# Dense matrices of a graph network: counts and first weight part in one product, three pairs of PSUM banks in turn

## The reference, cut to what matters

```python
h = relu(layernorm(x)); x = x + segment_sum(edge_weight[:, None] * h[src], dst)        # layer 0
h = relu(layernorm(x)); x = x + L1(h, edge_attr_2, src, dst)                           # MLP on every edge
h = relu(layernorm(x)); x = x + relu(segment_sum(edge_weight[:, None] * (h @ W)[src], dst) + bias)
h = relu(layernorm(x))
for l in range(3):                                                                     # layer 3
    out = segment_sum(h[src] + edge_attr_128, dst) + h
    z = gelu(layernorm(out @ W1[l].T + b1[l]))
    h = gelu(layernorm(z @ W2[l].T + b2[l]) + h)
x = x + h
```

## Time and profile before

| | us |
|---|---|
| median of 3 runs | 5626.27 |
| lowest, highest | 5624.34, 5633.94 |
| the profiled execution | 5629.7 |
| its span, first to last instruction | 5627.9 |
| the stage that builds the matrices | 168 to 1364 |
| layer 1, edge by edge | 1420 to 3990 |
| layer 2, sums by the stored weight matrix | 3990 to 4250 |
| the last three layers | 4250 to 5628 |

### The profile page before, as it was taken

One profiled execution on the slowest core, in us unless ns is written; L12 is line 12 of the kernel. 1 busy time (PEld: TensorE's weight loads), 2 busy tenths in 40 slices (PEclk: granted clock), 3 DMA queues, 4 the chain that ended last, 5 costly groups with the idle time before them and its releaser, 6 DMA issues.

```text
span 5627.9 us, 139608 instructions
## 1 busy us (share of the span) xinstructions
PE 4909.3 (87%) x42810; PEld 4173.0 (74%) x42810; DVE 3168.0 (56%) x9378; ACT 1754.6 (31%) x3785; POOL 2089.6 (37%) x2575
## 2 busy tenths in 40 slices
PE   1899999998888888888888888659998999999998
PEld 1799999998777777777777777459996666666665
DVE  7899999996555555555555555630003444444444
ACT  2555555555111111111111111210001444445445
POOL 6211111111777777777777777000000111111000
PEclk8999999999999999999999999879998999999999
DMA  6344444444555555555555555037775554554554
GB/s 169 148 205 198 193 191 205 205 199 166 132 132 132 132 133 133 131 133 132 133 132 132 133 131 133 12 137 294 291 292 188 189 183 176 189 183 178 188 183 160
DMA packets 464598, 943.57 MB, mean 168 GB/s; under 512 B 107346, under 2 KB 395970, under 8 KB 426898
## 3 DMA queue, kind: packets, MB, share of 16 engines
q1 hardware_dynamic: 187778, 696.55, 32.9%
q0 software_dynamic: 58304, 121.69, 9.0%
q10 hardware_dynamic: 218448, 124.48, 8.2%
HBM read 691.90 MB, written 250.56 MB: 167 GB/s over the span
## 4 chain that ended last, share of the span: by engine, by line
PE 65%; issue 10%; POOL 9%; DVE 5%; DMA 4%; ACT 3%; DVEq 3%; ACTq 1%; POOLq 0%; SPq 0%
PE ps L1142 20%; PE ps L975 10%; PE ps L997 10%; POOL BIG L695 9%; PE ps L960 7%; PE ps L1075 4%; DMA BIG<-table,IDX 4%; PE ps L1073 4%; PE ps L1085 4%; PE ps L958 2%; DVEq L378 2%; PE ps L1074 1%; ACT ACC L805 1%; PE ps L1029 1%; DVE BIG L1482 1%
## 5 line engine op out<-in xcount | busy, mean ns | idle before, releaser
L695 POOL DMA_INDIRECT BIG<-table,IDX x1664 | 1615.9, 971 | 535.5 <-issue 470.3
L1491 DVE TENSOR_TENSOR ACC<-ACC,ps 128x257 f32 x1664 | 702.4, 422 | 588.9 <-PE ps L1085 571.1
L1073 PE MATMUL ps<-T,BIG 128*128 x3328 | 698.7, 293 | 342.0 <-DMA BIG<-table,IDX 194.5
L1073 PEld LDWEIGHTS ps<-T,BIG 128*128 128x128 f32 x3328 | 539.8, 200 | 458.0 <-issue 449.7
L1085 PE MATMUL ps<-BIG 128*128 128x257 f32 x3328 | 808.3, 385 | 0.0
L1075 PE MATMUL ps<-BIG,ident 128*128 128x128 f32 x3328 | 771.4, 315 | 0.0
L975 PE MATMUL ps<-H,ACC 128*128 128x128 f32 x4802 | 690.5, 284 | 0.0
L1085 PEld LDWEIGHTS ps<-BIG 128*128 128x128 f32 x3328 | 615.3, 195 | 73.6
L833 ACT ACTIVATE IDX<-SRC 128x4 int32 (+1 forms) x416 | 85.1, 205 | 1827.9 <-PE ps L1075 1144.3
L960 PE MATMUL ps<-T,BIG 128*128 128x98 bf16 x9408 | 633.0, 206 | 0.0
L958 PE MATMUL ps<-BIG 128*128 128x98 bf16 x3136 | 569.4, 207 | 70.1 <-ACT ACC L805 53.2
(11 more groups left out here) (233 smaller groups left out, 6318.9 us busy)
## 6 DMA issues: line engine op xcount, KB each, us to landing
weight_mat<-ACC SPq DMA_DIRECT2D x49, 3136.0 KB, 9.3
BIG<-weight_mat SPq DMA_DIRECT2D x49, 3136.0 KB, 10.2
BIG<-count_mat SPq DMA_DIRECT2D x73, 1568.0 KB, 6.5
REL_WT<-count_mat SPq DMA_DIRECT2D x72, 1568.0 KB, 6.6
count_mat<-BIG SPq DMA_DIRECT2D x49, 1568.0 KB, 12.8
BIG<-rel_tab ACTq DMA_DIRECT2D x416, 128.0 KB, 3.1
BIG<-in_edge_attr SPq DMA_DIRECT2D x832, 64.0 KB
BIG<-in_edge_attr ACTq DMA_DIRECT2D x832, 64.0 KB
```

The costliest lines, as they stand in the source:

```text
L695: pool.indirect_dma_start(G[:, q * QUAD + u, :], None, tables[1], bass.IndirectOffsetOnAxis(ap=IDX[:, q, u:u + 1], axis=0)).then_inc(gathe ...
L1073: pe.matmul(to, DT[:, q % 2, u * P:(u + 1) * P], T1[:, b[q * QUAD + u], :], start=True, stop=False)
L1491: dve.tensor_tensor(to, to, PS[4 + u][:, 0:2 * F + 1], ALU.add).then_inc(slots_free, 1)
```

## The change

- The count product and the first weight product of a window become one product of 196 columns. For this the plain one-hots and the three weighted ones of a slot lie in one tile, OH[slot], of four planes of 8 x 100 columns; the moving operand takes planes 0 and 1, 98 columns from each, 800 elements apart. The other two weight parts follow, 98 columns each.
- A group's results lie in a pair of banks (1024 words): window j has 256 words, counts in the first 98, weights in the next 98. Two windows share a bank, and only the first of the two clears it (start=True).
- Three pairs are used in turn, q % 3; group 15 takes pair 1, so that group 0 of the next block finds pair 0. Before group q TensorE waits for both copies of group q-3 (of q-2 for groups 1 and 15).
- The sums of block_products go to the fourth pair (PS[6] and PS[7]) in place of PS[2] and PS[3].
- OH[0] and OA lie in T1, OH[1] in BIG, where before OR and OA lay in BIG and OW in T1.

```diff
 WG = -(-WINDOWS // P)
 QW = 4
 RING = 4
+BANKS = 3
+WSLOT = 2 * P
 GROUPS = WPB // QW
 HW = 8
 HOTS = WPB // HW
...
         LOF = BIG[:, 0:WG * P].rearrange("p (g j c) -> p g j c", j=WN, c=HALF)
         CODEF = BIG[:, WG * P:2 * WG * P].rearrange("p (g j c) -> p g j c", j=WN, c=HALF)
         WF = T1f[:, NP - WG * P:NP].rearrange("p (g j c) -> p g j c", j=WN, c=HALF)
-        def hots(flat, slots, c):
-            return flat.bitcast(BF16).rearrange("p (s k w c) -> p s k w c", s=HSLOTS, k=slots, w=HW)
-
-        OA_, at = of_big(NP, HSLOTS * HW * P // 2)
-        OR_, at = of_big(at, HSLOTS * HW * WPAD // 2)
+        HOT = (1 + PARTS) * HW * WPAD // 2
+        OH1_, at = of_big(NP, HOT)
         WST_, at = of_big(at, 2 * (2 + PARTS) * WPB * 2)
         assert at <= 2 * NP - WINDOWS
-        OW_ = T1f[:, WINDOWS:WINDOWS + HSLOTS * PARTS * HW * WPAD // 2]
-        assert WINDOWS + HSLOTS * PARTS * HW * WPAD // 2 <= NP
-        OA, OR, OW = hots(OA_, 1, P), hots(OR_, 1, WPAD), hots(OW_, PARTS, WPAD)
+        OH0_ = T1f[:, WINDOWS:WINDOWS + HOT]
+        OA_ = T1f[:, WINDOWS + HOT:WINDOWS + HOT + HSLOTS * HW * P // 2]
+        assert WINDOWS + HOT + HSLOTS * HW * P // 2 <= NP
+        OA = OA_.bitcast(BF16).rearrange("p (s w c) -> p s w c", s=HSLOTS, w=HW)
+        OH = [flat.bitcast(BF16).rearrange("p (k w c) -> p k w c", k=1 + PARTS, w=HW) for flat in (OH0_, OH1_)]
         WST = WST_.bitcast(BF16).rearrange("p (a k w j) -> p a k w j", a=2, k=2 + PARTS, w=WPB)
         RELH0 = WG * WN * RUN * 3
...
         cmp = T2[:, 2 * SG * P:2 * SG * P + SG * (BLOCKS - 1)].rearrange("p (g b) -> p g b", b=BLOCKS - 1)
-        PS = [ctx.enter_context(nc.psum_tensor(f"ps{k}", [P, 512], FP32)) for k in range(8)]
+        PP = [ctx.enter_context(nc.psum_tensor(f"ps{k}", [P, 1024], FP32)) for k in range(4)]
+        PS = [PP[k // 2][:, k % 2 * 512:(k % 2 + 1) * 512] for k in range(8)]
         waits_passed = sem("waits_passed")
...
             return [(c, CHUNK if c < CHUNKS else 1, c % 2) for c in range(C1)]
+        def group_banks(q):
+
+            return PP[1 if q == GROUPS - 1 else q % BANKS]
+
+        def copies_needed(q):
+
+            return q + (2 if q in (1, GROUPS - 1) else 1)
+
         def again(v):
             return not isinstance(v, int) or v >= 2
...
             def store_block(b, par, i):
-                sp.wait_ge(group_out, (b + 1) * GROUPS + 4)
+                sp.wait_ge(group_out, (b + 1) * GROUPS + BANKS)
                 sp.dma_start(weight_mat[b, :, :], WB[par]).then_inc(mat_out[par], 16)
                 sp.dma_start(count_mat[b, :, :], CB[par]).then_inc(mat_out[par], 16)
...
                 which, n = k % 3, min(4 * P, WINDOWS - k // 3 * 4 * P)
                 act.wait_ge(wturned, k + 1)
                 act.activation((LO, CODE, WW)[which][:, k // 3 * 4 * P:k // 3 * 4 * P + n], PS[k % 4][:, 0:n], ACT.Copy).then_inc(wcopied, 1)
-            act.sem_inc(group_out, 4)
-            act.sem_inc(count_out, 2)
+            act.sem_inc(group_out, BANKS)
+            act.sem_inc(count_out, BANKS)
             act.sem_inc(wsum_used, 2)
...
                 act.wait_ge(wsum_ps, b + 1)
                 for q in range(GROUPS):
                     act.wait_ge(group_ps, b * GROUPS + q + 1 + RING)
-                    for pair, to, done in ((q % 2, CB[par], count_out), (4 + q % 4, WB[par], group_out)):
+                    for k, to, done in ((0, CB[par], count_out), (1, WB[par], group_out)):
+                        of = group_banks(q).rearrange("p (w z) -> p w z", z=WSLOT)[:, :, k * WCOLS:(k + 1) * WCOLS]
                         act.activation(
                             to.rearrange("p (h d) -> p h d", d=P)[:, :, q * QW * WN:(q + 1) * QW * WN].rearrange("p h (w j) -> p h w j", j=WN),
-                            PS[pair][:, 0:QW * WCOLS].rearrange("p (w h j) -> p h w j", w=QW, j=WN), ACT.Copy).then_inc(done, 1)
+                            of.rearrange("p w (h j) -> p h w j", j=WN), ACT.Copy).then_inc(done, 1)
             def copied_blocks():
                 block_pairs(act, group_copies)
                 act.wait_ge(mat_out[0], 32 * 25)
...
                     g, half = q // 2, q % 2
                     pe.wait_ge(hot_ready, (b + 2) * HOTS + g + 1)
-                    pe.wait_ge(count_out, b * GROUPS + q + 1)
-                    pe.wait_ge(group_out, b * GROUPS + q + 1)
+                    pe.wait_ge(count_out, b * GROUPS + copies_needed(q))
+                    pe.wait_ge(group_out, b * GROUPS + copies_needed(q))
                     for j in range(QW):
                         w = half * QW + j
-                        one = OA[:, g % HSLOTS, 0, w, :]
-                        pe.matmul(PS[q % 2][:, j * WCOLS:(j + 1) * WCOLS], one, OR[:, g % HSLOTS, 0, w, 0:WCOLS], start=True, stop=True)
-                        for k in range(PARTS):
-                            mm = pe.matmul(PS[4 + q % 4][:, j * WCOLS:(j + 1) * WCOLS], one, OW[:, g % HSLOTS, k, w, 0:WCOLS],
-                                           start=(k == 0), stop=(k == PARTS - 1))
+                        one, hot = OA[:, g % HSLOTS, w, :], OH[g % HSLOTS]
+                        to = group_banks(q)[:, j * WSLOT:j * WSLOT + 2 * WCOLS].rearrange("p (k c) -> p k c", k=2)
+                        pe.matmul(to, one, hot[:, 0:2, w, 0:WCOLS], start=(j % 2 == 0), stop=False)
+                        for k in range(1, PARTS):
+                            mm = pe.matmul(to[:, 1, :], one, hot[:, 1 + k, w, 0:WCOLS], start=False, stop=(j % 2 == 1 and k == PARTS - 1))
                     mm.then_inc(group_ps, 1)
                     products(q)
...
                 def some(q):
                     if q == lead:
-                        pe.wait_ge(group_out, (b + 1) * GROUPS + 4)
+                        pe.wait_ge(group_out, (b + 1) * GROUPS + BANKS)
                         pe.wait_ge(wsum_used, b + 1)
                     if q >= lead:
                         for h in range((q - lead) * share // 2, (q - lead + 1) * share // 2):
-                            mm = pe.matmul(PS[2 + par][:, 0:F], WB[par][:, h * P:(h + 1) * P], H[:, h, :], start=(h == 0), stop=(h == BLOCKS - 1))
+                            mm = pe.matmul(PS[6 + par][:, 0:F], WB[par][:, h * P:(h + 1) * P], H[:, h, :], start=(h == 0), stop=(h == BLOCKS - 1))
                         if q == GROUPS - 1:
                             mm.then_inc(wsum_ps, 1)
                 assert (GROUPS - lead) * share // 2 == BLOCKS
...
             def added(b, par):
                 dve.wait_ge(wsum_ps, b + 3)
-                dve.tensor_tensor(X[:, b, :], X[:, b, :], PS[2 + par][:, 0:F], ALU.add).then_inc(wsum_used, 1)
+                dve.tensor_tensor(X[:, b, :], X[:, b, :], PS[6 + par][:, 0:F], ALU.add).then_inc(wsum_used, 1)
             def block_statistics(b):
                 wait_alone(dve, wsum_used, b + 3)
...
                         block_statistics(b - 2)
                     dve.wait_ge(group_ps, b * GROUPS + (2 * g + RING - 2))
-                    dve.tensor_tensor(four(OR[:, k, 0, :, :]), across(iotab1, WPAD), along(par, 1, g, WPAD), ALU.is_equal).then_inc(hot_plain, 1)
-                    dve.tensor_tensor(four(OA[:, k, 0, :, :]), across(iotab, P), along(par, 0, g, P), ALU.is_equal)
+                    dve.tensor_tensor(four(OH[k][:, 0, :, :]), across(iotab1, WPAD), along(par, 1, g, WPAD), ALU.is_equal).then_inc(hot_plain, 1)
+                    dve.tensor_tensor(four(OA[:, k, :, :]), across(iotab, P), along(par, 0, g, P), ALU.is_equal)
                     dve.wait_ge(hot_plain, b * HOTS + g + 1)
                     for part in range(PARTS):
-                        last = dve.tensor_tensor(four(OW[:, k, part, :, :]), four(OR[:, k, 0, :, :]), along(par, 2 + part, g, WPAD), ALU.mult)
+                        last = dve.tensor_tensor(four(OH[k][:, 1 + part, :, :]), four(OH[k][:, 0, :, :]), along(par, 2 + part, g, WPAD), ALU.mult)
                     last.then_inc(hot_ready, 1)
             def built_blocks():
```

## The result

| | us |
|---|---|
| before, median of 19 runs (18 of 5622.30 to 5633.94, one of 9327.87) | 5626.12 |
| after, median of 19 runs (5609.95 to 5618.94) | 5615.14 |
| ratio, 95% interval | 0.998, 0.9973 to 0.9987 |
| forecast, range | 5621, 5605 to 5634 |
| the profiled execution after, its span | 5609.95, 5608.1 |

The changed kernel is 11.0 us faster, where 5.4 had been forecast.

A forecast was written before the change was run, and what follows sets the result against it. The prediction took a 24.25 us block cycle, TensorE's groups 2 to 13 then VectorE's pairs 0 and 1, to bound the stage. From 5626.27 us it took 5.4 for the wide product, all else nil: about 5621, range 5605 to 5634.

The forecast's parts named there:

- Who ends the wait before group 2: TensorE's hole before group 2 in each block: VectorE's pair 1 ends it, not the ScalarE copy the profile names.
- The wide product, 5.4 us: Windows of groups 2 to 13, blocks 1 to 48: one product fewer saves 2.35 ns in each of 2304 windows.
- The line through two widths: TensorE product cost from 98 and 384 columns: 0.4175 ns per column plus 2.3 ns per product, so 84.1 ns for 196.
- Two runs of columns: Wide product's moving operand, two runs 800 elements apart: no cost taken; a stop between runs left to the slow rival.
- ScalarE's steps of 256 words: ScalarE's copies across a pair of banks: price unknown, up to a doubling, covered by idle time; nothing taken.
- The ring, "Cost: nil": TensorE's waits for copies, three pairs of banks replacing two and four: relief worth nothing, new waits covered.
- the rival with the copy: Hole before group 2 is partly the ring's: 8.5 us more gain, 5612 us; chance 0.08.
- VectorE's operations in other places: One-hots and weighted ones moved between T1 and BIG: place doesn't matter to VectorE's 6.21 us, nothing taken.
- The slow rival: Wide product: the second run of columns stops the stream; with 14 ns, 27 us slower, 5653 us; chance 0.08.
- the load rival: TensorE windows: weight loads set the rate, so 99.5 us would go, 5527 us; chance 0.01.
- the larger fixed part: TensorE products: fixed part larger than the line says, up to 21 us gain, 5605 us; chance 0.05.
- same: Whole kernel: within about 0.2% (11 us) of before, 5615 to 5637.5 us; chance 0.76.

The follow-up runs named there:

- e2: The kernel before, with group 1 made to wait for one more copy than it needs, the value group 2 waits for; 5621.95 us, ratio 0.9989.
- e4: The changed kernel with group 2's wait for the weights copy one value lower, so computed again behind the one-hots wait; 5618.44 us, ratio 0.9984.
- e5: The changed kernel with a ring two deep everywhere instead of three and the one-hots waited for last; 5615.35 us, ratio 0.9978.
- e6: The changed kernel with the 49 block-sum products shared out otherwise, more of them after groups 13, 14 and 15; 5580.48 us, ratio 0.9919.
- e3: The changed kernel with the wide product split into two of 98 columns again, new banks and waits kept; 5619.49 us, ratio 0.9984.
- e8: The kernel before with only e6's moved block-sum products; 5582.74 us, ratio 0.9922.
- e11: The kernel of e9 once more on another chip; 5567.63 us, ratio 0.9894.
- e1: The kernel before, with TensorE's waits ahead of a group reordered, the two copies first and the one-hots last; 5619.62 us, ratio 0.9985.
- e9: The changed kernel with e6's moved sums, e1's wait order and GpSimd's memset of ACC held until VectorE's second statistics; 6150.29 us, ratio 0.991.

## Why the prediction was right or wrong

- *Who ends the wait before group 2*: right. It was VectorE and not the copy that the view of waits names. The last block's rows had told them apart; e2, e4, e5 and e6 confirm it. What lay between VectorE and the first product was missed.
- *The wide product, 5.4 us*: right. 170 ns per window; by the periods of e3 and the changed kernel 0.10 us per block, 5 us in 48 blocks. The line through two widths held for a third between them.
- *Two runs of columns*: no cost, neither for reading the moving operand nor for ScalarE's steps of 256 words (copies 498 and 494 ns, as before).
- *The ring, "Cost: nil"*: this step failed, by +8 us of gain. The depth is indeed worth nothing (e5). But rewriting the waits also changed which computations stand behind them, 0.17 us per block. The prediction had the number in hand: it noted that TensorE started 0.24 us after VectorE's end where block 0 had 0.06 (the rows of block 0 stand under Experiments, not in the earlier trace rows), and gave the 0.18 between to the rival with the copy, at a chance of 0.08. The size of that rival (8.5 us, 5612) was right and its mechanism wrong. What wasn't looked at is the sequencer's own rows on the lines of the waits.
- *VectorE's operations in other places*: 607 and 565 ns for the multiplications by slot, against 587 before, so the mean is the same; its two pairs take 695.26 - 689.05 = 6.21 us as before.
- *The slow rival, the load rival, the larger fixed part*: none of them came. One argument against the slow rival was weaker than it looked: the 35 turns of line 927 don't take 213 ns each. Their starts lie 213 to 252 ns apart up to 97.6 us and 168 to 247 ns after, with a mean of 215; nor does any row show the half clock for them (the view gives 1.00 for 93 to 101 us). That two runs of columns cost nothing was shown by the changed kernel, not by that row.
- The chances: 5615.14 is 0.2% below before and on the edge of "same". Faster had 0.15. The gain is twice the forecast, and that it still lies in the range is in part luck: the lower end, 5605, had been set for a larger fixed part of the product, which didn't come, and not for the sequencer. Had the sequencer's part been seen, the forecast would have been 5626.3 - 5.4 - 8.2, 5613, and the larger part of the chance would have lain on faster.

Open: stages and periods give 13 us less, the medians 11.0; the interval of the ratio (7 to 15 us) covers both.

## What to carry to other kernels

Where an engine waits for several semaphores, wait last for the one that comes last, and let nothing that must be computed stand behind it; rows of the sequencer on the waits' own lines show whether something does. A ring's depth is worth looking at only after the releaser's end has been compared with the start in two places where the engines are timed differently. When a stage gets shorter, look at what the next one now meets: here a memset that had just missed another engine's instruction took back 10 us of 44.

## What the runs showed of the hardware

- A VectorE TENSOR_SCALAR on 49 fp32 elements took 10.36 us beside a GpSimd MEMSET of 10.6 us, and 0.19 us away from it. The Trainium skill (SBUF — State Buffer, Who interferes with whom) says that a VectorE instruction in a two-port mode and GpSimd shut each other out for the whole instruction, and counts tensor_scalar among those that can enter such a mode. The trace agrees: the instruction ended with the memset. Other VectorE instructions ran beside the same memset at their usual length: in e8 (memset 1321.40 to 1332.00) a RECIPROCAL of 49 elements took 0.47 us and a SCALAR_TENSOR_TENSOR 0.21, as in e11 ahead of the memset. Not tried: the same instruction in a form without that mode.
- A register computation and a semaphore instruction behind a wait on TensorE cost 0.17 us together (period 24.25 against 24.08 us in e1), though their rows are 32 and 51 ns; the computation alone 0.08 us (e4).
- The Trainium skill (Advanced Engine Details and Errata, PSUM Cachelines) warns that non-contiguous patterns slow matmuls. For a moving operand of two runs of 98 bf16 columns, 800 elements apart, with a contiguous result, the trace shows no slowing: 84 ns for 196 columns, by the 170 ns of a window less two products of 43.
- One chip of those used needs 10% more for the same kernel (6202 against 5628 us). e9 and e11 are one kernel on two chips: 514 of the 589 us between their spans (6151.3 and 5562.7) lie in the loop of gathers, 65 ahead of the stage's first sums, and the period of the stage treated here is the same on both (22.99 us).
